# The output projection of the last stage as three F32R products of halves

## The reference

```
q = x @ q_w.T + q_b                      # 16 heads of 16
xd = conv1d(x, stride 2, per channel);  k, v = xd @ k_w.T + k_b, xd @ v_w.T + v_b
out = softmax(q k^T / 4) v               # per head, 2048 queries, 1024 keys
x = layernorm(x + out @ out_w.T + out_b)
h = layernorm(x) * gamma + beta          # the feed-forward block's own norm
y = silu(h @ w1 + fc1_bias)              # 256 -> 1024, w1 and w2 dequantized
x = layernorm(x + x_ffn), x_ffn = x + 0.5 * (y @ w2 + fc2_bias)
```

## Time and profile before

| | us |
|---|---|
| median of 3 runs | 3921.28 |
| lowest and highest | 3910.47, 3923.24 |
| profiled execution, own time | 3923.83 |
| its span, first to last instruction | 3922.0 |

### The profile page before, as it was taken

The page is one execution under the profiler, slowest core; times in us unless marked ns, Lnnn a source line. Parts: engine busy times, 40 slices in busy tenths (PEclk is TensorE's granted clock), DMA queues, the critical chain, the costliest instruction groups (busy, mean ns, idle before and its releaser), DMA issues. The chain is left out here.

```text
span 3922.0 us, 76603 instructions
## 1 busy us (share of the span) xinstructions
PE 3836.8 (98%) x22744; PEld 1997.9 (51%) x22744; DVE 3324.9 (85%) x4142; ACT 2613.2 (67%) x4969; POOL 844.7 (22%) x553
## 2 busy tenths in 40 slices
PE   9969999999999999999999999999999999999998
PEld 5633333333333333333333333333334799999998
DVE  9869998999899899989989998999996677777775
ACT  4428887888788788878878887887887333343343
POOL 6521200000000000000000000000001687787775
PEclk9979999999999999999999999999999999999999
DMA  8991124105112410511241051124111222222220
GB/s 297 342 202 52 53 44 60 34 27 70 35 33 43 61 34 27 70 35 32 43 61 34 27 70 34 34 42 62 34 31 63 76 86 81 69 86 77 73 86 27
DMA packets 315395, 269.39 MB, mean 69 GB/s; under 512 B 156594, under 2 KB 225202, under 8 KB 315315
## 3 DMA queue, kind: packets, MB, share of 16 engines
q1 hardware_dynamic: 304818, 261.47, 27.0%
q10 hardware_dynamic: 9376, 2.89, 0.8%
q0 software_dynamic: 1120, 4.19, 0.4%
HBM read 157.30 MB, written 110.10 MB: 68 GB/s over the span
## 5 line engine op out<-in xcount | busy, mean ns | idle before, releaser
L749 DVE TENSOR_REDUCE half_max<-first_ps 128x2 f32<-128x1024 f32 x2038 | 2401.3, 1221 | 289.4 <-PE first_ps L585 285.7
L712 ACT ACTIVATE probs<-score_ps 128x512 f32<-128x512 f32 x4096 | 2114.7, 603 | 586.6 <-PE score_ps L610 541.3
L610 PE MATMUL score_ps<-q_s,k_s 49*128 49x512 f32 x4096 | 1444.7, 477 | 31.9 <-DMA q_s<-max_row 13.4
L610 PEld LDWEIGHTS score_ps<-q_s,k_s 49*128 49x128 f32 x4096 | 574.7, 185 | 1291.6 <-ACT probs L712 1164.7
L620 PE MATMUL pv_ps<-probs,v_s 128*32 128x512 f32 x8192 | 1101.1, 610 | 0.0
L585 PE MATMUL first_ps<-k_s,q_s 48*128 48x512 f32 x4076 | 904.3, 422 | 15.2 <-PEq L189 10.5
L858 POOL TENSOR_TENSOR num<-num,rden 128x1024 f32<-128x1024 f32 x2 | 4.7, 2364 | 2586.8 <-DMA rden<-rden_d 2586.8
L1033 ACT ACTIVATE act_f<-fc_ps,b 128x512 f32<-128x512 f32 x256 | 174.9, 684 | 474.1 <-PE fc_ps L986 472.0
L585 PEld LDWEIGHTS first_ps<-k_s,q_s 48*128 48x128 f32 x4076 | 409.0, 188 | 62.0 <-issue 11.9
L1110 DVE CAST a_hi<-act_f 128x512 fp32r<-128x512 f32 x256 | 236.0, 922 | 150.6 <-ACT act_f L1033 150.1
L1162 POOL TENSOR_TENSOR a_lo<-act_f,a_hi 128x512 fp32r<-128x512 f32 x256 | 339.5, 1331 | 86.2 <-DVE a_hi L1110 86.2
(11 more groups left out here) (109 smaller groups left out, 2537.6 us busy)
## 6 DMA issues: line engine op xcount, KB each, us to landing
o_d<-o_sb SPq DMA_DIRECT2D x128, 256.0 KB, 2.1
q_s<-q_hi_d SPq DMA_DIRECT2D x504, 64.0 KB, 2.1
x_t<-x_c_in SPq DMA_DIRECT2D x32, 512.0 KB, 5.6
q_hi_d<-q_hi SPq DMA_DIRECT2D x32, 512.0 KB, 4.5
q_lo_d<-q_lo SPq DMA_DIRECT2D x32, 512.0 KB, 4.8
x_res<-x_in SPq DMA_DIRECT2D x32, 512.0 KB
num<-o_d SPq DMA_DIRECT2D x64, 256.0 KB
rden<-rden_d SPq DMA_DIRECT2D x64, 256.0 KB
```

What stands on the lines that cost most here:

```text
L610: pe.matmul(bank(s, u)[:, :], k_s[g][at, a, t * P:(t + 1) * P], q_s[g][at, a, :], start=True, stop=True).then_inc(scored, 1)
L712: nc.scalar.activation(probs[s % 2][:, u, :], bank(s, u)[:, :], ACT.Exp).then_inc(exped, 1)
L749: dve.reduce_max(half_max[g % 2][:, :, a * TT + t, keys], first_ps[keys][:, :, :], AX.X)\
```

## The change

`wo` and `num` are split as the feed-forward weights are. New tiles wo_hi, wo_lo, num_hi and num_lo are in F32R. POOL makes wo_hi and wo_lo once, ahead of the rounds. ACT makes num_hi of block n+2 in round n, two copies of 128x512 between the Silus of tiles 6 and 7. DVE makes num_lo of block n+2 in the same round, two subtractions between the cast of tile 6 and hidden_lo. PE sums three products for each of the eight old ones. The projection of block 1, in round 0, keeps the old form, and so does that of block 0. To make room the tile for the last denominators goes, and they use y_out of buffer 1.

```diff
+        wo_hi, wo_lo = sb("wo_hi", [P, CC, C], F32R), sb("wo_lo", [P, CC, C], F32R)
+        num_hi, num_lo = sb("num_hi", [P, CC, QB], F32R), sb("num_lo", [P, CC, QB], F32R)
...
-        dens = sb("last_dens", [P, QB])
+        dens = y_out[1][:, 0:QB // C, :].rearrange("p t c -> p (t c)")
...
+            def project_split(n):
+                pe.wait_ge(wo_up, 2)
+                pe.wait_ge(nlo_up, CC * n - CC)
+                pe.wait_ge(r1_up, 1 + 2 * n)
+                terms = [(a, w, c) for c in range(CC) for a, w in ((num_hi, wo_hi), (num_hi, wo_lo), (num_lo, wo_hi))]
+                for t in range(TT):
+                    for i, (a, w, c) in enumerate(terms):
+                        last = pe.matmul(proj_ps[t // 2][:, t % 2, :], a[:, c, t * P:(t + 1) * P], w[:, c, :],
+                                         start=i == 0, stop=i == len(terms) - 1)
+                    if t % 2:
+                        last.then_inc(proj_mm, 1)
...
                     if f == 0 and r.has(1):
-                        project_out(n + 1, r.buf(1))
+                        if r.has(-1):
+                            project_split(n + 1)
+                        else:
+                            project_out(n + 1, r.buf(1))
...
+            def num_upper(n, j):
+                act.wait_ge(attn_up, n + 1)
+                act.wait_ge(proj_mm, 2 * n)
+                for c in range(CC):
+                    nc.scalar.activation(num_hi[:, c, :], num[j][:, c, :], ACT.Copy).then_inc(nhi_up, 1)
...
+                    if f == FC - 2 and r.has(2):
+                        num_upper(n + 2, r.buf(2))
...
+            def num_lower(n, j):
+                for c in range(CC):
+                    dve.wait_ge(nhi_up, CC * n - 2 * CC + c + 1)
+                    dve.tensor_tensor(num_lo[:, c, :], num[j][:, c, :], num_hi[:, c, :].bitcast(F32), ALU.subtract)\
+                        .then_inc(nlo_up, 1)
...
                 tile(6)
+                if r.has(2):
+                    num_lower(n + 2, r.buf(2))
                 if r.has(1):
                     hidden_lo(n + 1)
...
+            pool.tensor_copy(wo_hi[:, :, :], wo[:, :, :]).then_inc(wo_up, 1)
+            pool.wait_ge(wo_up, 1)
+            pool.tensor_tensor(wo_lo[:, :, :], wo[:, :, :], wo_hi[:, :, :].bitcast(F32), ALU.subtract).then_inc(wo_up, 1)
             rounds(pool, body)
```

More of the change, by code:

```diff
@@ L894, in finish @@
         out_stored = [sem(f"out_stored{i}") for i in two]
-        rden_up = sem("rden_up")
+        rden_up, wo_up, nhi_up, nlo_up = sem("rden_up"), sem("wo_up"), sem("num_hi_up"), sem("num_lo_up")
         fc1_mm, act_up, ahi_up, alo_up, fc2_mm, r3_up, y_up = (
@@ L947, in _ @@
                 sp.sem_inc(given, 1)
-            sp.dma_start(dens[:, :], all_dens[DEN - 1]).then_inc(den_loaded, 16)
+            sp.dma_start(dens, all_dens[DEN - 1]).then_inc(den_loaded, 16)
             def last_rden():
                 sp.wait_ge(rden_up, 1)
-                sp.dma_start(all_rdens[DEN - 1], dens[:, :]).then_inc(rden_stored, 16)
+                sp.dma_start(all_rdens[DEN - 1], dens).then_inc(rden_stored, 16)
                 sp.wait_ge(rden_stored, 16)
@@ L1149, in last_rden @@
                 dve.wait_ge(den_loaded, 16)
-                dve.reciprocal(dens[:, :], dens[:, :]).then_inc(rden_up, 1)
+                dve.reciprocal(dens, dens).then_inc(rden_up, 1)
             rounds(dve, body, last_rden)
```

## The result

| | us |
|---|---|
| changed kernel, median of 5 runs | 4019.90 (4014.27 to 4028.46) |
| kernel before, median of 5 runs | 3914.91 (3910.47 to 3923.24) |
| ratio | 1.0267, 95% interval 1.0256 to 1.0278 |
| profiled span, before and after | 3922.0, 4012.5 |

The change makes the kernel slower by 105 us. The forecast was +66 us (3987), with 3912 to 4010 as its range. The direction and the stall were foretold. The time lies 10 us above the range, since a second loss, the falling clock, came on top of the stall; the forecast had put it at nothing, and it stood among the rivals with 6 in 100. The forecast was added to 3921.28 us, the median of the three runs known then; with five runs that median is 3914.91, so the miss is 39 us (105 less 66) and not 33. Ratios compare fast runs alone; one run, of the kernel before with x_b last, was slow at 14465 us and enters no ratio.

A forecast was written before the change was run, and what follows sets the result against it. PE was taken to bound the kernel. 29 rounds by 2.74 us of stall (79.5), plus 3.7 for round 0, less 17.1 saved, gave +66 us on 3921: 3987 us, own range 3975 to 4005, 8-in-10 range 3912 to 4010.

The forecast's parts named there:

- the falling clock: Rival: each last-stage stall halves PE's clock for one tile, 1.54 us by 29, 45 us more: 4032 us; chance 0.06.
- What bounds the kernel: Last stage: PE busy 831.27 of 832.00 us; a microsecond off PE is one off the time unless data comes late.
- What is taken off PE: Projection in rounds 1 to 30: 24 F32R products at 2.88 us replace 3.45 us, 0.57 a round, 17.1 us saved.
- ACT: Two num_hi copies between the Silus of tiles 6 and 7: 1.1 us taken, no cost on the path by itself.
- DVE and POOL take turns: Around num_lo, ahead of h_lo: first num_lo waits for a_lo, x_b goes next, then second num_lo; h_lo ends 3421.86.
- no contention: Rival: POOL does not hold up num_lo ahead of h_lo, so nothing stalls: 3905 us; chance 0.14.
- DVE keeps its turn: Rival: second num_lo slips in ahead of x_b; stall about 0.5 us eats the 0.57: about 3921 us; chance 0.08.
- The size of the stall: PE's wait for h_lo, rounds 1 to 29: 2.74 us a round, ends 2.6 and 3.0, 79.5 us in all.
- The shift of POOL's run: POOL's run lies 0.26 us earlier against the Silu of tile 6, cutting the stall from 3.00 to 2.74 us.
- Round 0: No fc2 work as cover; the same turns put h_lo's end at 3072.15 in place of 3068.48: 3.7 us more.

The follow-up runs named there:

- warm PE: Changed kernel with ten throwaway 128x512 products on PE ahead of its wait for h_lo, against the kernel before: 3992.46 us, ratio 1.0193.

## Where the prediction was right, and where it failed

- **What bounds the kernel.** Right. With num_lo gone, less work on PE became 16 us less of time.
- **What is taken off PE.** The piece is right: the chain has 2.87 us for the 24 products, against 2.88 foretold, and an unhindered round is 0.56 us shorter. Its worth was sized too high. 17.1 us took for granted that nobody is late for a faster PE; the rounds without a stall show 0.38 to 0.40 us, 11 to 12 us in all, and the medians 14 and 16 with 6 to either side. The four passes of the Trainium skill, FP8 and Floating Point Precision, section TensorE Precision Notes, would have made it an estimated 28.8 us. No run comes near that, and the measurement decides.
- **ACT.** Right: two num_hi take 1.14 us, and the version with the old product and all the new work beside it has the rounds of the kernel before, 26.94 us.
- **DVE and POOL take turns.** Right, read from one pair of casts. The five ends above repeat it with instructions of another kind to 0.01 us, and the run with x_b moved shows that the length of the POOL instruction let in is what counts. The rivals "no contention" and "DVE keeps its turn" fall.
- **The size of the stall.** 2.74 foretold, 2.83 us with a warm PE. The shift of POOL's run came nearly as foretold: h_lo ends 7.59 us after the Silu of tile 6 begins, against 7.52 foretold with the shift and 7.78 without. Round 0 grew by 3.7 us in the changed kernel, as foretold. The warm PE gave +76 us where the sum of stall and saving has +66 (1.0193, with 7 us to either side), and its trace says where the 10 are: 29 by 0.09 = 3 us of stall, 3 us in the rounds 2 to 4 before they are steady (29.64, 31.25 and 29.38 us in place of 29.20), and 4 us of the throwaway products themselves.
- **The step that failed: the clock.** The sum put it at nothing, and I made it a rival of 6 in 100 with the words that "the stall has a PE without a gap on both sides". That is no argument from a row: the trace of before had a fall in round 0 and no gap of 2 to 3 us in a busy PE to compare with. 25 of the 30 rounds fell, for 1.5 us each. The price of one fall was well sized (1.54 foretold), and 38 us are counted in the rows; 27 us are left of it in the trace and 29 in the medians, since the next stall is often shorter. The rival's 4032 us was the nearest of my cases.
- **The whole.** By the traces the stage is 98 us longer than before, from its first fc_ps product to the end (978.6 and 880.6 us): 66 as forecast, 27 of clock, and 5 to 6 of stall. The other 7 of the 105 are not in these two traces. The profiled run of the changed kernel is the fastest of its five and that of the kernel before is above its five, so part of it may be scatter; the rest is open.
- **The range** took in a kept turn on the fast side, and ended at 4010 on the slow side. The clock would have wanted its upper end at 4032.
- **The shift, once more.** It was near the truth for the forecast, but the same way of thinking made the expectation for one num_lo miss by 33 us. Once PE waits for DVE and DVE for POOL, the place of POOL's run is a result of the loop and cannot be kept from the profile of before.

## What to carry to other kernels

Before work is put on an engine that has time left, look at what stands behind it in that engine's list and which instruction of another engine it may have to let pass: here 1.3 us of subtraction with 1.05 us of room became 2.8 us of stall, through one POOL addition that nobody was waiting for. Put such work behind what the bound engine waits for, in one instruction rather than two, and move the long instruction that can wait out of the way. Each of the moves alone still lost 22 us or more, and together they gained. What is then taken off the bound engine is worth its full length only as long as the others can follow: here 0.57 us a round became 0.40. Where a stall appears on a TensorE that had none, price the clock with it and not as an alternative to it.

## What the runs showed of the hardware that was not expected

- PE gaps of 1.9 to 3.1 us (5.1 in round 1), once in a round of 30 us that is otherwise full, were followed by a granted clock of 1.2 GHz in 25 of 30 rounds; in the five others, after gaps of 1.8 to 1.9 us, it stayed at 2.4. But other gaps of 1.88 us were followed by a fall some microseconds later, so the length of the gap alone doesn't decide. Ten throwaway products in the gap kept the clock at 1.00.
- An instruction of DVE that has waited for POOL needs only 0.54 to 0.55 us after the release, for 128x512 with both inputs in SBUF. Its whole record was 1.60 or 2.89 us, and the shortest num_lo, in the run with x_b behind the a_lo of tile 6, took 0.68 us.
- The start of PE after h_lo came 0.12 us after its end in the changed kernel and 0.04 us in the one with a warm PE, some 2 us over the stage. The warm PE need not be the reason: in rounds 1 and 30 of the changed kernel, which stand outside the loop of four rounds, it is 0.05 us after a gap of 5.1 and 1.8 us.
